# Eight-chunk Mamba and expert layer on one core: the convolution's fourth tap goes to ScalarE inside the bank, one of 13 products per chunk from GpSimd to VectorE, and two SiLU stretches become one

## The chip, the cores and the metric

One core of one Trainium2 chip. The metric is the device time of one execution in microseconds, over repeated executions. Three were taken of the kernel before: 1012.83 us in the median (1012.59 to 1013.26).

## What is computed

The input `x` has 4096 tokens of 256 numbers, in fp32 throughout. The reference is a layer norm, a Mamba block with its own RMS norm and two residual sums, then a layer norm and a mixture of eight expert networks, each for its own 512 tokens:

```python
xs, res = jnp.split(_rmsnorm(x, rms_w) @ W_in, 2, axis=-1)      # 512 channels each
xs = silu(conv_1d_depthwise(xs, conv_w, taps=4, causal) + conv_b)
dt, Bm, Cm = jnp.split(xs @ W_x, [512, 528], axis=-1)           # 16 states
dt = softplus(dt @ W_dt)
h = exp(A * dt) * h + dt * Bm * xs      # per token, 512 channels x 16 states
y = sum_n(h * Cm) * silu(res)
x = x + residual + y @ W_out
x = x + (silu(n @ w1[e]) * (n @ w3[e])) @ w2[e]                 # n = layernorm(x), e = token // 512
```

## The kernel before

**Chunks and tiles.** The tokens are cut into E = 8 chunks of TC = 512. One iteration `i` scans chunk `i`, and beside it runs the "front" of chunk `i+1` (input projection, convolution, B and C, dt) and the "back" of chunk `i-1` (gating, output projection, expert network). The scan of a chunk is Q = 32 tiles `q` of NG = 2 rows each. A row is 128 channels by 512 tokens for one state: ScalarE writes exp(A dt) to one of two PSUM banks `ebank` (line 806), VectorE runs the recurrence over it (line 664), in place in one of RING = 4 slots of `ring`, which held B times u (u = dt times xs). GpSimd multiplies the result by C (`hc`, line 513), and TensorE transposes and sums that into `ybank` (line 1133). The product B times u of a tile is made by GpSimd (line 499) for the 13 tiles in `POOL_BU` (line 34) three tiles ahead, and by VectorE (line 649) for the rest, just before the tile's scan. GpSimd reads u from SBUF, VectorE from the PSUM bank `ubank`, which ScalarE copies (line 820).

**The order of work.** Each engine executes its own list in order. The function `run` (line 306) goes over the iterations and their 32 tiles; after each tile's own work (`group`) it issues the jobs that the engine's table names for that tile. The tables are `table0` for iteration 0 and `table` for the later ones. TensorE takes its jobs from PLAN, FIRST and LAST (lines 112 to 145), and its `group` handles the tile LAG = 3 before. A job that waits holds up everything behind it on its engine, the exponentials of ScalarE and the transposes of TensorE among them.

**Banks.** Four PSUM banks `gbank` serve all other products. A loop at line 166 gives every job of the plan the bank whose last use is estimated to end first (the last number of an entry). `wait_free` waits until the job before in that bank was read, `wait_full` until the product is there.

**The convolution.** For each of the four groups `d` of 128 channels, TensorE projects into a bank ("IN"), ScalarE copies that to `xpre` (`before_conv`, line 842, two groups at tile 1 and two at tile 2), TensorE multiplies three shifted views of `xpre` by diagonal matrices into another bank ("CV", `convolve`, line 1225), and VectorE adds the fourth tap and writes `xs` (`convolved`, line 632, tiles 3, 4, 6, 6; tiles 15 to 18 in iteration 0). At tile 8 ScalarE loads the SiLU table, turns the four `xs` into SiLU in place and loads the exponential's table again (`silus`, line 871).

**Other jobs that are named below.** ScalarE: `residual` at tile 6 (line 928, four activations into the banks of "M"), `y_read` (line 894), `softplus` (line 905), `gate_silus` at tile 20 (line 1003). VectorE: `hidden(f)` at tiles 20 to 23 (line 749), which reads the bank "UP" f, `dt_of` (line 622), `gated` (line 671), `m_stats` (line 694), `x_stats` (line 616). GpSimd: `u_of` (line 481). TensorE: "DT" d (`dt_in`), "UP" f (`expand`), "DOWN" (`contract`, `contract_on`). The SiLU of the gate input `sres` (`res_silu`, line 867) runs in `gate_silus` from iteration 1 on. Those of chunks 0 and 1 run in iteration 0: that of chunk 0 in `silus_first` at tile 19, that of chunk 1 in `silus_res` at tile 24 with two table loads of its own.

## Time and profile before

| | |
|---|---|
| median of 3 executions | 1012.83 us |
| the profiled execution | 1013.09 us, of it a span of 1011.3 us in the profile |
| TensorE matmul / weight load busy | 91% / 59% |
| VectorE busy | 91% |
| ScalarE busy | 69% |
| GpSimd busy | 90% |
| mean granted TensorE clock | 0.973 of full speed |
| chain that ended last, by engine | VectorE 35%, issue 18%, TensorE 11%, GpSimd 10%, ScalarE 9% |

The three busy engines each stand near 90% over the whole span, which holds a start of about 42 us and an end of about 45 us in which only some of them have work. "Idle before" in a row is the time for which the engine did nothing before the group, and what ended it. "L664" is line 664 of the kernel.

### The profile page before, as it was taken

What the parts mean: (1) busy time and instruction counts of PE and PEld (TensorE: products, weight loads), DVE (VectorE), ACT (ScalarE), POOL (GpSimd) and SP (SyncE); (2) the same over time, 40 slices, a digit from 0 to 9 for tenths busy, and PEclk for the clock granted to TensorE, in tenths of its full rate; (3) what the DMA queues carried; (4) which work ended last, traced back from release to release, by engine and by line L of the source; (5) the groups of instructions that cost most, each with busy time, mean ns of one, the idle gap of its engine ahead of it and who ended that gap; (6) DMA issues with size and microseconds to landing.
All of it is one profiled execution on the core that took longest, in us unless ns stands there. A gap on an engine that the chain in (4) does not pass through costs nothing.

```text
span 1011.3 us, 13001 instructions
## 1 busy us (share of the span) xinstructions
PE 924.9 (91%) x4160; PEld 591.8 (59%) x4160; DVE 923.8 (91%) x1003; ACT 697.0 (69%) x1188; POOL 909.1 (90%) x499
## 2 busy tenths in 40 slices
PE   6888978999999999999999999999999997669978
PEld 4445545655756556655756557655656655555745
DVE  5789889999999999999999999999999999899941
ACT  4556777778758877778758867687758876567610
POOL 1499899999999999999999999999999999999910
PEclk9999998999999999999999999999999999779989
DMA  5590135010841039010851039110750028100200
GB/s 170 198 348 21 42 131 246 1 65 3 329 172 43 24 129 372 2 66 0 312 190 42 25 112 343 47 65 1 288 214 25 21 99 320 42 21 1 87 22 21
DMA packets 42852, 117.86 MB, mean 117 GB/s; under 512 B 8608, under 2 KB 27040, under 8 KB 32672
## 3 DMA queue, kind: packets, MB, share of 16 engines
q1 hardware_dynamic: 40928, 116.99, 30.9%
q8 instruction: 33, 0.54, 0.2%
q10 hardware_dynamic: 1856, 0.04, 0.1%
q14 instruction: 35, 0.29, 0.1%
HBM read 110.21 MB, written 6.82 MB: 116 GB/s over the span
## 4 chain that ended last, share of the span: by engine, by line
DVE 35%; issue 18%; PE 11%; POOL 10%; ACT 9%; DVEq 0%; POOLq 0%; ACTq 0%
DVE ring L664 24%; DVE ring L649 8%; POOL hc L513 7%; PE gbank L1070 4%; PE gbank L1084 3%; POOL ring L499 3%; ACT ebank L806 2%; PE ybank L1133 2%; ACT hb L1008 1%; DVE dt_ L629 1%; ACT L1011 1%; ACT L1004 1%; PE gbank L1194 1%; DVE hb L753 1%; DVE sres L676 1%
## 5 line engine op out<-in xcount | busy, mean ns | idle before, releaser
L664 DVE TENSOR_TENSOR_SCAN ring<-ebank,state,ring 128x512 f32<-128x512 f32 x512 | 623.5, 1267 | 28.0 <-ACT ebank L806 19.7
L513 POOL TENSOR_TENSOR hc<-ring,c_all 128x1024 f32<-128x1024 f32 x255 | 599.0, 2368 | 22.6 <-DMA c_all<-bc_kept 11.0
L806 ACT ACTIVATE ebank<-dt_,a_neg 128x512 f32<-128x512 f32 x512 | 349.6, 689 | 218.5 <-DVE ring L664 216.7
L1133 PEld LDWEIGHTS ybank<-ident,hc 128*128 128x128 f32 x2048 | 236.8, 143 | 105.2 <-issue 62.8
L1133 PE MATMUL ybank<-ident,hc 128*128 128x128 f32 x2048 | 262.0, 277 | 24.7 <-POOL hc L513 12.4
L499 POOL TENSOR_TENSOR ring<-b_all,u 128x1024 f32<-128x1024 f32 x103 | 243.9, 2368 | 2.3 <-ACT state L810 2.3
L649 DVE TENSOR_TENSOR ring<-b_all,ubank 128x1024 f32<-128x1024 f32 x151 | 180.5, 1195 | 1.7 <-ACT ubank L820 1.7
L1070 PE MATMUL gbank<-xT,w 128*128 128x512 f32 x320 | 150.7, 605 | 12.3 <-DVE hb L753 11.4
L1070 PE MATMUL gbank<-xT,w_a 128*128 128x512 f32 x256 | 118.5, 601 | 6.2 <-DVE dt_ L629 4.0
L1070 PE MATMUL gbank<-xs,w_a 128*128 128x512 f32 x224 | 101.0, 595 | 0.0
L1070 PEld LDWEIGHTS gbank<-xT,w 128*128 128x128 f32 x320 | 57.1, 193 | 64.5 <-issue 51.5
L1084 PE MATMUL gbank<-w2s,hb 128*128 128x256 f32 x336 | 84.4, 394 | 2.5 <-DVE hb L753 2.5
L1070 PEld LDWEIGHTS gbank<-xT,w_a 128*128 128x128 f32 x256 | 46.6, 192 | 52.3 <-issue 43.6
L1070 PE MATMUL gbank<-xpre,cdiag 128*128 128x512 f32 x168 | 76.0, 595 | 0.7 <-ACT xpre L825 0.7
L1084 PEld LDWEIGHTS gbank<-w2s,hb 128*128 128x128 f32 x336 | 60.5, 193 | 18.2 <-issue 11.9
L1070 PEld LDWEIGHTS gbank<-xs,w_a 128*128 128x128 f32 x224 | 41.0, 190 | 46.0 <-issue 46.0
L1084 PE MATMUL gbank<-wout,sres 128*128 128x256 f32 x224 | 52.9, 391 | 11.3 <-ACT gbank L937 11.3
L1084 PEld LDWEIGHTS gbank<-wout,sres 128*128 128x128 f32 x224 | 42.7, 196 | 18.4 <-issue 12.8
L1070 PEld LDWEIGHTS gbank<-xpre,cdiag 128*128 128x128 f32 x168 | 30.1, 189 | 32.0 <-issue 32.0
L486 POOL TENSOR_TENSOR u<-dt_,xs 128x512 f32<-128x512 f32 x31 | 39.6, 1279 | 0.9 <-DVE dt_ L629 0.9
L1070 PE MATMUL gbank<-xs,wbc 128*32 128x512 f32 x64 | 29.0, 595 | 0.0
L1078 PE MATMUL gbank<-ident,xin 128*128 128x128 f32 x120 | 18.6, 297 | 9.2 <-ACT xin L833 8.0
(135 smaller groups left out, 752.1 us busy)
## 6 DMA issues: line engine op xcount, KB each, us to landing
b_all<-bc_kept SPq DMA_DIRECT2D x32, 1024.0 KB, 7.2
c_all<-bc_kept SPq DMA_DIRECT2D x32, 1024.0 KB, 8.3
w<-in_L_ffn_w_dram SPq DMA_DIRECT2D x16, 640.0 KB, 4.9
w_a<-wc_kept SPq DMA_DIRECT2D x7, 1024.0 KB, 4.8
w_a<-win_kept SPq DMA_DIRECT2D x6, 1024.0 KB, 8.9
w2s<-in_L_ffn_w_dram SPq DMA_DIRECT2D x8, 640.0 KB, 4.5
xin<-in_L_attn_x_dram SPq DMA_DIRECT2D x9, 512.0 KB, 3.5
x<-in_L_attn_x_dram SPq DMA_DIRECT2D x7, 512.0 KB, 7.2
```

The costliest lines, as they stand in the source:

```text
L486: u_ok.by(e.tensor_tensor(u[:, d, :], dt_[:, d, :], xs[:, d, :], ALU.mult))
L499: bup_ok.by(e.tensor_tensor(ring[:, q % RING, :, :], b_all[:, n:n + NG, :], u[:, d, :].unsqueeze(1).broadcast_to([P, NG, TC]), ALU.mult))
L513: ch_ok.by(e.tensor_tensor(hc[:, q % HC, :, :], ring[:, q % RING, :, :], c_all[:, n:n + NG, :], ALU.mult))
L629: read_out(e.scalar_tensor_tensor(dt_[:, d, :], bank[:, :], 0.0, xpre[:, d, HALO:HALO + TC], ALU.max, ALU.add), i, "DT", d)
L649: bud_ok.by(e.tensor_tensor(ring[:, q % RING, :, :], b_all[:, n:n + NG, :], ubank[:, :].unsqueeze(1).broadcast_to([P, NG, TC]), ALU.mult))
L664: h_ok.by(e.tensor_tensor_scan(row, ebank[j % 2][:, :], row, initial=state[:, q, n:n + 1], op0=ALU.mult, op1=ALU.add))
L676: read_out(e.tensor_tensor(mine, bank[:, :], mine, ALU.mult), i, "YT", d)
L806: e_ok.by(e.activation(ebank[j % 2][:, :], dt_[:, d, :], ACT.Exp, scale=a_neg[:, d, k:k + 1]))
L1070: last = e.matmul(out_ap, a, b, start=(n == 0), stop=(n == len(terms) - 1))
L1078: return e.matmul(bank[:, cols(b)], src, ident[:, :], is_transpose=True, start=(b == 0), stop=(b == NT - 1), skip_group_check=True)
L1084: last = e.matmul(out_ap, a, b, start=False, stop=(n == len(terms) - 1), skip_group_check=True)
L1133: last = e.matmul(ybank[:, cols(b)], hc[:, q % HC, n, cols(b)], ident[:, :], is_transpose=True, start=(k == 0 and n == 0 and b == 0), stop ...
```

## The change

`convolved` moves from VectorE to ScalarE. `before_conv` now also scales the bank in place by the fourth tap after copying it, TensorE adds the other three products on top in the same bank (so "CV" no longer takes a bank of its own, and the plan's "CV" entries only say when it is read), and ScalarE copies the sum to `xs`. Tile 7 leaves `POOL_BU`. In iteration 0 `silus_res` is gone; its SiLU runs in `silus` of iteration 1. The plan and the tables are written anew around that. The core of the diff:

```diff
-    POOL_BU = (1, 4, 6, 7, 10, 12, 15, 18, 19, 22, 25, 26, 29)
+    POOL_BU = (1, 4, 6, 10, 12, 15, 18, 19, 22, 25, 26, 29)
...
         PLAN = [
-            (0, "front", "IN", 0, 1.4), (0, "front", "IN", 1, 2.2), (0, "front", "IN", 2, 2.4), (1, "front", "IN", 3, 0.5),
-            (2, "front", "CV", 0, 2.7), (3, "front", "CV", 1, 5.2), (4, "back", "YT", 3, 5.4), (4, "front", "CV", 2, 8.2),
+            (0, "front", "IN", 0, 2.4), (0, "front", "IN", 1, 0.5), (1, "front", "IN", 2, 1.4), (2, "front", "IN", 3, 2.2),
+            (2, "front", "CV", 0, 2.7), (3, "front", "CV", 1, 5.2), (4, "back", "YT", 3, 5.4), (4, "front", "CV", 2, 9.2),
...
-            (18, "back", "TAIL", 0, 23.5), (18, "scan", "YT", 1, 21.5), (18, "back", "UP", 0, 21.3), (20, "back", "UP", 1, 22.2),
-            (21, "back", "UP", 2, 22.4), (22, "back", "UP", 3, 22.7), (23, "front", "DT", 1, 25.3), (24, "back", "UP", 4, 23.4),
+            (18, "back", "TAIL", 0, 23.5), (18, "scan", "YT", 1, 21.5), (18, "back", "UP", 0, 21.3), (19, "back", "UP", 1, 22.2),
+            (21, "back", "UP", 2, 22.4), (22, "front", "DT", 1, 25.3), (23, "back", "UP", 3, 22.7), (24, "back", "UP", 4, 23.4),
...
         for i in range(-1, E + 1):
+            added = {k: until for _, _, name, k, until in plan(i) if name == "CV"}
...
+                if name == "CV":
+                    continue
...
+                    if name == "IN" and i >= 0:
+                        made[b] += 1
+                        PLACE[of, "CV", k] = b, made[b]
+                        out_at[b] = i * Q + added[k]
...
-            table = [(2, "scan", u_of(ND - 1)), (8, "back", back), (16, "handed", hand_on), (16, "front", u_of(0)),
-                     (20, "next", front), (29, "front", u_of(1)), (31, "front", u_of(2))]
-            table0 = [(5, "late", u_of(1)), (6, "late", u_of(2)), (10, "late", u_of(3)), (22, "handed", hand_on),
-                      (23, "next", front), (26, "front", u_of(0)), (27, "front", u_of(1)), (31, "front", u_of(2))]
+            table = [(0, "scan", u_of(ND - 1)), (8, "back", back), (16, "front", u_of(0)), (19, "handed", hand_on),
+                     (20, "next", front), (27, "front", u_of(1)), (31, "front", u_of(2))]
+            table0 = [(5, "late", u_of(1)), (6, "late", u_of(2)), (10, "late", u_of(3)), (23, "handed", hand_on),
+                      (25, "next", front), (26, "front", u_of(0)), (29, "front", u_of(1)), (31, "front", u_of(2))]
...
-            def convolved(d):
-                def job(c, i):
-
-                    u_ok.wait(e, c - 1, d + 1)
-                    bank = wait_full(e, i, "CV", d)
-                    read_out(e.scalar_tensor_tensor(xs[:, d, :], xpre[:, d, HALO:HALO + TC], cw[:, d, HALO:TAPS], bank[:, :], ALU.mult, ALU.add),
-                             i, "CV", d)
-                return job
...
-            table = [(3, "front", convolved(0)), (4, "back", gated(ND - 1)), (4, "front", convolved(1)),
-                     (6, "front", convolved(2)), (6, "front", convolved(3)), (8, "back", m_stats), (14, "scan", gated(0)),
-                     (17, "front", dt_of(0)), (20, "next", x_stats), (20, "scan", gated(1)), (20, "back", hidden(0)),
-                     (20, "back", hidden(1)), (20, "back", hidden_tail), (21, "back", hidden(2)), (22, "back", hidden(3)),
-                     (23, "back", hidden(4)), (24, "front", dt_of(1)), (27, "front", dt_of(2)), (28, "ahead y", gated(2)),
+            table = [(4, "back", gated(ND - 1)), (8, "back", m_stats), (15, "scan", gated(0)), (17, "front", dt_of(0)),
+                     (20, "next", x_stats), (20, "scan", gated(1)), (20, "back", hidden(0)), (20, "back", hidden_tail),
+                     (20, "back", hidden(1)), (21, "back", hidden(2)), (23, "back", hidden(3)), (23, "back", hidden(4)),
+                     (24, "front", dt_of(1)), (27, "ahead y", gated(2)), (27, "front", dt_of(2)), (30, "scan y", gated(2)),
...
             table0 = [(0, "late", fed), (2, "late", dt_of(1)), (7, "late", dt_of(2)), (9, "late", dt_of(3)),
-                      (15, "front", convolved(0)), (16, "front", convolved(1)), (17, "front", convolved(2)),
-                      (18, "front", convolved(3)), (19, "next", x_stats), (19, "scan", gated(0)), (22, "scan", gated(1)),
+                      (19, "scan", gated(0)), (20, "next", x_stats), (23, "scan", gated(1)), (28, "front", dt_of(0)),
...
-                        move("IN", d, i, xpre[:, d, HALO:HALO + TC])
+                        bank = wait_full(e, i, "IN", d)
+                        e.activation(xpre[:, d, HALO:HALO + TC], bank[:, :], ACT.Copy)
+                        read_out(e.activation(bank[:, :], bank[:, :], ACT.Copy, scale=cw[:, d, HALO:TAPS]), i, "IN", d)
+                return job
+
+            def convolved(d):
+                def job(c, i):
+                    u_ok.wait(e, c - 1, d + 1)
+                    move("CV", d, i, xs[:, d, :])
                 return job
...
                 xs_silus(c, i)
-                e.preload_act_table_set(LOG_EXP)
-
-            def silus_res(c, i):
-                e.preload_act_table(ACT.Silu)
-                res_silu(c, i)
+                if i == 1:
+                    res_silu(c - 1, i - 1)
                 e.preload_act_table_set(LOG_EXP)
...
-            table = [(1, "front", before_conv(0, 1)), (2, "front", before_conv(2, 3)), (3, "back", y_read(ND - 1)),
-                     (6, "back", residual), (8, "front", silus), (9, "back", m_copy), (10, "scan", y_read(0)),
+            table = [(1, "front", before_conv(0, 1)), (2, "front", before_conv(2, 3)), (3, "front", convolved(0)),
+                     (3, "back", y_read(ND - 1)), (4, "front", convolved(1)), (6, "front", convolved(2)), (6, "back", residual),
+                     (7, "front", convolved(3)), (8, "front", silus), (9, "back", m_copy), (10, "scan", y_read(0)),
...
-            table += [(24, "back", down_on(0)), (26, "back", down_on(1)), (28, "back", down_out(0)), (30, "ahead", residual),
+            table += [(24, "back", down_on(0)), (25, "back", down_on(1)), (30, "back", down_out(0)), (30, "ahead", residual),
...
-                      (19, "front", res(0, 1)), (19, "scan", y_read(1)), (20, "front", res(2, 3)), (22, "front", bc_read),
-                      (24, "front", softplus(0)), (24, "front", silus_res), (26, "front", softplus(1)), (26, "scan", y_read(2)),
+                      (19, "front", silus_first), (19, "scan", y_read(1)), (20, "front", res(0, 1)), (21, "front", res(2, 3)),
+                      (22, "front", bc_read), (25, "front", softplus(0)), (26, "front", softplus(1)), (27, "scan", y_read(2)),
...
-                    bank = wait_free(e, i, "CV", d)
-                    filled(product(bank[:, :], [(cdiag[:, d, k, :], xpre[:, d, k:k + TC]) for k in range(TAPS - 1)]), i, "CV", d)
+                    bank = gbank[PLACE[i, "CV", d][0]]
+                    filled(add_on(bank[:, :], [(cdiag[:, d, k, :], xpre[:, d, k:k + TC]) for k in range(TAPS - 1)]), i, "CV", d)
...
-            table += [(26, "back", contract_on(0)), (29, "back", contract_on(1))]
+            table += [(27, "back", contract_on(0)), (28, "back", contract_on(1))]
```

With these entries the loop that gives out banks puts "DT" 2 of a later iteration in the bank that "UP" 3 leaves, as before.

## Rows read from the trace of the kernel before

**Rows 1.** Busy time in stretches; columns: stretch, length, PE, PEld, DVE, ACT, POOL, clock.

```profile
347.60:462.00 114.40, 111.65 (x511) 70.79 (x510) 112.47 (x120) 87.06 (x149) 113.75 (x61) 1.00 0.33 126
...
577.10:692.20 115.10, 112.11 (x503) 70.67 (x501) 112.24 (x120) 86.49 (x149) 113.51 (x62) 0.99 0.34 125
```

**Rows 2.** Groups by line: busy us, mean ns of one, idle before them.

```profile
L664 DVE TENSOR_TENSOR_SCAN ring<-ebank,state,ring 128x512 f32<-128x512 f32 x512 | 623.5, 1267 | 28.0 <-ACT ebank L806 19.7 <-POOL ring L499 4.9
L513 POOL TENSOR_TENSOR hc<-ring,c_all 128x1024 f32<-128x1024 f32 x255 | 599.0, 2368 | 22.6 <-DMA c_all<-bc_kept 11.0 <-DVE ring L664 9.4 <-PE ybank L1133 2.1
...
L499 POOL TENSOR_TENSOR ring<-b_all,u 128x1024 f32<-128x1024 f32 x103 | 243.9, 2368 | 2.3 <-ACT state L810 2.3
...
L649 DVE TENSOR_TENSOR ring<-b_all,ubank 128x1024 f32<-128x1024 f32 x151 | 180.5, 1195 | 1.7 <-ACT ubank L820 1.7
...
L637 DVE SCALAR_TENSOR_TENSOR xs<-xpre,cw,gbank 128x512 f32<-128x512 f32 x28 | 20.0, 732 | 0.0
...
L1024 ACT ACTIVATE xs<-gbank,cw 128x512 f32<-128x512 f32 x4 | 2.7, 687 | 2.8 <-PE gbank L1070 2.8
```

**Rows 3.** Waits from 347.6 to 462 us: who waited for whom, us, times, longest.

```profile
ACT ebank L806 <- DVE ring L664: 24.7, 38, 2.9
...
DVE ring L664 <- ACT ebank L806: 1.2, 2, 0.7
...
DVE ring L664 <- POOL ring L499: 0.3, 1, 0.3
```

**Rows 4.** VectorE's timeline, a later iteration: start, us, what, idle before.

```profile
366.33 0.68 DVE L753 TENSOR_TENSOR hb<-hb,gbank 128x512 f32<-128x512 f32 x1
...
394.02 4.79 DVE L664 TENSOR_TENSOR_SCAN ring<-ebank,state,ring 128x512 f32<-128x512 f32 x4
...
416.04 1.38 DVE L637 SCALAR_TENSOR_TENSOR xs<-xpre,cw,gbank 128x512 f32<-128x512 f32 x2
417.34 2.45 DVE L664 TENSOR_TENSOR_SCAN ring<-ebank,state,ring 128x512 f32<-128x512 f32 x2
```

**Rows 5.** ScalarE's timeline beside them.

```profile
395.39 0.69 ACT L806 ACTIVATE ebank<-dt_,a_neg 128x512 f32<-128x512 f32 x1 [2.14 <-DVE ring L664]
...
397.13 1.06 ACT L825 ACTIVATE xpre<-gbank 128x512 f32<-128x512 f32 x2
398.08 1.46 ACT L806 ACTIVATE ebank<-dt_,a_neg 128x512 f32<-128x512 f32 x2
...
414.54 2.03 ACT L937 ACTIVATE gbank<-x,kept 128x256 f32<-128x256 f32 x4
416.50 1.28 ACT L806 ACTIVATE ebank<-dt_,a_neg 128x512 f32<-128x512 f32 x2
```

**Rows 6.** TensorE's timeline beside them.

```profile
353.83 1.98 PE L1070 MATMUL gbank<-xT,w 128*128 128x512 f32 x4 [1.75 <-DVE hb L753]
...
365.14 3.60 PE L1070 MATMUL gbank<-xs,w_a 128*128 128x512 f32 x8
...
392.32 5.32 PE L1070 MATMUL gbank<-xT,w_a 128*128 128x512 f32 x12
397.47 1.04 PE L1133 MATMUL ybank<-ident,hc 128*128 128x128 f32 x8
```

**Rows 7.** Iteration 0: VectorE's timeline.

```profile
69.69 1.22 DVE L649 TENSOR_TENSOR ring<-b_all,ubank 128x1024 f32<-128x1024 f32 x1 [1.70 <-ACT ubank L820]
...
139.66 4.81 DVE L664 TENSOR_TENSOR_SCAN ring<-ebank,state,ring 128x512 f32<-128x512 f32 x4 [4.39 <-ACT ebank L806]
```

**Rows 8.** Iteration 0: GpSimd's timeline, the first piece after a wait.

```profile
125.32 4.71 POOL L513 TENSOR_TENSOR hc<-ring,c_all 128x1024 f32<-128x1024 f32 x2 [0.66 <-DVE ring L664]
```

**Rows 9.** Iteration 0: ScalarE's timeline, the SiLU that moves.

```profile
135.65 1.91 ACT L869 ACTIVATE sres<-sres 128x2048 f32<-128x2048 f32 x1
```

**Rows 10.** TensorE's timeline where the iteration of 115.1 us begins.

```profile
582.90 3.38 PE L1070 MATMUL gbank<-xT,w 128*128 128x512 f32 x4 [2.10 <-DVE hb L753]
```

**Rows 11.** Waits from 806 to 965 us (iteration 7).

```profile
DVE ring L664 <- POOL ring L499: 2.4, 2, 1.6
```

More of the change, by code:

```diff
@@ new lines, in _ @@
+            table0 = [(0, "late", fed), (2, "late", dt_of(1)), (7, "late", dt_of(2)), (9, "late", dt_of(3)),
+                      (19, "scan", gated(0)), (20, "next", x_stats), (23, "scan", gated(1)), (28, "front", dt_of(0)),
+                      (28, "front", dt_of(1)), (29, "front", dt_of(2)), (30, "scan", gated(2)), (30, "front", dt_of(ND - 1))]
+            last = [(2, "back", last_c), (3, "back", gated_last), (3, "back", add_rows("M", 0, x1a_ok)),
+                    (4, "back", add_rows("M", 1, x1a_ok)), (4, "back", x1_stats), (4, "back", normal_last),
+                    (5, "back", turned_last), (5, "back", hidden_last), (12, "back", add_last)]
```

36 lines of the change are left out of this document (16 added, 20 removed), and 6 rows, old and new, of the table FIRST.

## The prediction

> **What bounds the kernel now.** I read the span in stretches first. In a later iteration GpSimd is busy for 113.75 us of 114.40, VectorE for 112.47 and TensorE for 111.65, ScalarE for 87.06 [rows 1]. So three engines are full and one has room. The waits of that iteration say how much slack is left: VectorE waits for ScalarE's exponentials for 1.2 us in two places (0.7 and 0.5, behind the two SiLU stretches) and for a product of GpSimd for 0.3 [rows 3]; GpSimd waits for nothing. VectorE and GpSimd bound an iteration together, so relief of one alone is worth nothing. The change relieves both, and pays with ScalarE.
>
> ScalarE's room is not free time. It has two banks for its exponentials, so each has a moment at which it must begin. In the timelines, a scan starts at 394.02 and the exponential two rows on starts 1.37 us later, at 395.39 [rows 4, 5]; a scan starts 0.84 us after its exponential (416.50 to 417.34) [rows 4, 5]. Scans follow each other at 1.18 us (4.79 for four, less 0.1 overlap) [rows 4]. Two scans give 2.37 us; 1.37 + 0.84 of them are taken. A job between two pairs of exponentials is free only up to about 0.75 us, plus whatever else VectorE does between those scans.
>
> **Prices.** Rows overlap by about 0.1 us at their ends, so steps are shorter than durations.
> - VectorE's fourth tap: two in 1.30 us (416.04 to 417.34), 0.65 each [rows 4]; its group has 28 at 732 ns [rows 2].
> - A product of B and u: 2368 ns on GpSimd, 1195 ns on VectorE [rows 2]; steps of 2.32 and 1.23, since the scan behind it waits for its end.
> - ScalarE's plain copy: two in 0.95 us (397.13 to 398.08), 0.48 each [rows 5]. Its copy with a per-channel scale, from a bank to SBUF, took 687 ns [rows 2]; the exponential, which has such a scale and writes to a bank, 0.69 [rows 5]. The in-place scaling of a bank isn't in the trace. It lies between 0.48 (plain copy) and 0.69 (no overlap); I take 0.60, by the scaled rows less the overlap.
>
> The rows show no difference between a bank and SBUF as the destination. The Trainium skill (ScalarE: Activation LUTs, "Step-by-step: what each stage is for") holds that ScalarE writes faster to PSUM than to SBUF; by that the 28 scalings would come nearer to 0.48, and the stalls below would shrink by about 0.2 us per iteration.
>
> **An iteration from 1 to 6, by load.** VectorE loses 4 × 0.65 = 2.6 us, gains 1.23, and saves 0.1 where `gated(0)` now stands behind a product: −1.47. GpSimd loses 2.32. ScalarE gains 4 × (0.60 + 0.48) = 4.3 us, which its 27 us of idle time could hold [rows 1]. TensorE issues the same matmuls; that three of them add to a filled bank I cost at nothing, bounded by 0 and 0.1 us. SP's transfers wait for the same events; the one behind the last "DOWN" comes one tile earlier.
>
> **The same iteration, by order.** Let 0 be the first scan of tile 0 (394.02).
> - TensorE first. VectorE read "UP" 4 at 366.33 [rows 4]. `hidden(3)` now stands just ahead of it and nothing of it is left at tile 22, so `hidden(3)` begins near 365.9 and ends near 366.5. "DT" 2 needs its bank; it began at 365.14 before [rows 6] and so begins 1.4 us later. From there to the projection at 392.32 TensorE showed no pause [rows 6], so "IN" 0 begins at 393.7, that is −0.3.
> - With 0.43 us per matmul of 512 columns (12 in 5.15) and 0.87 for a tile's eight transposes [rows 6]: "IN" 1 is full at 3.2, "IN" 2 at 5.7, "IN" 3 (behind one more tile than before) at 8.4, "CV" 0 at 11.0, "CV" 1 at 14.4.
> - ScalarE, tile 1: exponentials until 3.1, then two pairs of copy and scale, 2.16 us, until 5.3. The next exponential should begin by 5.1: **stall 0.14**.
> - Tile 2: the second pair waits for "IN" 3 and ends at 9.5 instead of 8.8. Tile 3's scans could begin at 9.7, and begin at 10.3: **stall 0.64**.
> - Tile 3: `convolved(0)` waits for "CV" 0 until 11.0, then `y_read`: 12.0, 0.1 late: **stall 0.08**.
> - Tile 6: `convolved(2)` (0.48) stands ahead of `residual` (1.96, 414.54 to 416.50 [rows 5]), where VectorE has 1.23 us of cover instead of the 1.30 of two taps: **stall 0.55**.
> - Tile 7: `convolved(3)` and the copy of `ubank` fit below the product of tile 8.
>
> New stalls 1.41 against −1.47, and the 0.3 us of waiting for GpSimd goes, as GpSimd has 2.3 us less to do: −0.3 per iteration, six times **−1.9 us**. Late next is ScalarE, held by TensorE.
>
> **Iteration 0.** GpSimd reaches `u_of(1)` one product (2.3 us) earlier, so VectorE's 1.70 us at 69.69 goes [rows 7]. VectorE's 4.39 us at 139.66 are `silus_res`: a SiLU of 1.91 us [rows 9] between two table loads. It goes too [rows 7]. But from 125.32 on GpSimd has work without a long pause until the iteration's end [rows 8], so that what VectorE gains at 139.66 shows only as far as the ring lets it lead. Of 1.70 + 4.39 = 6.1 us at least the first part comes out, since it lies before GpSimd's full stretch, and at most the whole. I take the middle, **−4.0**, bounds −1.7 and −6.1.
>
> **Iteration 1** gets that SiLU into the stretch at tile 8, which VectorE waits out already: **+1.8**, or nothing if VectorE arrives late.
>
> **Iteration 7** has no front. VectorE waits for GpSimd for 2.4 us, 1.6 of it for the product of tile 7 [rows 11]. VectorE makes that itself in 1.23, and the other 0.8 goes: about −1.1. A pause for TensorE's output projection takes 0.2 back: **−0.9**. LAST keeps each engine's order: 0.
>
> Sum: −4.0 + 1.8 − 1.9 − 0.9 = −5.0. From the profiled execution's 1013.09 us: 1008.1. That one stands 0.26 above the median of 1012.83, so **1007.8**; its own range is 1005 to 1010.5 (the scaling's bounds are ±1.2, iteration 0 ±2.2).
>
> **Rivals** (0.2%, 2 us, is about what a measurement of this kernel can tell from no change).
> - TensorE on time (0.20): it makes up the 1.4 us before tile 0. Then "IN" 3 and "CV" 0 are full when wanted and only 0.14 + 0.57 remain: −1.0 per iteration, **1003.6**. For it: "IN" 3 would come 0.7 us before it is wanted. Against: no pause in [rows 6].
> - GpSimd's pace (0.05): if ScalarE's stalls fall where VectorE would wait anyway, each iteration gains the full 2.3 us, **about 996**. Against it, VectorE is full too [rows 1].
> - Slower, by TensorE's clock (0.15). Every iteration TensorE waits for `hidden(0)`: 1.75 us at 353.83, and the four matmuls behind took 1.98 [rows 6]. Once it waited 2.10 us and they took 3.38 [rows 10], a granted clock of 1.2 in place of 2.4 GHz, and that iteration took 115.1 us instead of 114.4 [rows 1]. The change puts a second wait (1.4 us, "DT" 2) behind the first. If the clock falls in each of six iterations, the 0.7 us come back, and some 1.0 more, as ScalarE now waits for "IN" 3 in order: +1.4 each, 8.3 − 3.1 = 5.2: **1018**. It decides from 0.5 us per iteration.
> - Nothing (0.15): the stalls eat the gain of every iteration, and what iteration 0 saves comes back with iteration 1's SiLU: **1011 to 1013**. Part of the change would still do what it says.
> - The forecast has 0.45.
>
> The Trainium skill (TensorE: Matmul & The Clock Gate, "What's actually happening") says that the array runs at half rate by default and only activity releases it. The trace agrees: [rows 10] is the slow stretch behind a wait. [...]
>
> The range 1003.0 to 1013.0 takes in the forecast, TensorE on time and nothing, and leaves out 0.2. Faster 0.70 (forecast, the two faster rivals), same 0.15, slower 0.15.
>
> **What would show it.** No row of a scalar-tensor product into `xs` on VectorE; 28 scalings in a bank near 0.69 us; 95 products on GpSimd, 159 on VectorE. VectorE's waits for `ebank` in an iteration rise from 1.2 to about 2.6 us, with new ones near tiles 3 and 7; ScalarE's copies to `xpre` wait for TensorE; GpSimd waits for VectorE by some 2 us. A period near 114.1. The forecast is wrong if the period falls to 113.4 (TensorE on time), or rises with a clock below 1.00 in each iteration.

## The result, and the profile after it

The changed kernel took 1025.79 us (median of 4 runs, 1022.86 to 1026.95) against 1013.05 us for the kernel before beside it, a recorded ratio of 1.0103 with a 95% interval of [1.0081, 1.0126]: **slower by 1%**, where 1007.8 us and faster had been forecast. (The quotient of the two medians, of four runs each, is 1.0126, at the upper end of that interval; all ratios below are the recorded ones.) The profiled execution took 1022.86 us with a span of 1021.1, so it is 9.8 us longer in span than the profiled one before (1011.3).

In the comparisons below the kernel before took anything from 1012.5 to 1018.3 us, most of it probably in the first chunk (last section), so kernels are compared by ratio within one batch, and by the period of the later iterations.

The page of the changed kernel, busy time and the chain that ended last (by engine, by line):

```profile
PE 926.7 (91%) x4160; PEld 591.3 (58%) x4160; DVE 918.0 (90%) x983; ACT 721.3 (71%) x1242; POOL 890.5 (87%) x491
...
PE 58%; issue 11%; ACT 10%; DVE 10%; POOL 9%; DMA 0%; DVEq 0%; POOLq 0%; ACTq 0%
PE gbank L1072 23%; PE gbank L1086 17%; PE ybank L1135 13%; DVE ring L662 6%; POOL hc L520 5%; POOL ring L506 3%; ACT ebank L801 2%; DVE ring L647 2%; PE gbank L1080 2%; ACT hb L1008 2%; DVE hb L751 1%; ACT L1011 1%; ACT L1004 1%; ACT yt L902 1%; PE gbank L1196 1%
```

The chain now runs through TensorE for 58% of the span; through VectorE for only 10%. L1072 are the projections, L1086 the accumulating products (the convolution, the output projection and the down projection), L1135 the sums of the 16 states into y.

The changed kernel's groups by line. The scalings in a bank are there (28, 666 ns), GpSimd has 95 products and VectorE 159, and no row of VectorE writes `xs` from a bank, as the change says:

```profile
L506 POOL TENSOR_TENSOR ring<-b_all,u 128x1024 f32<-128x1024 f32 x95 | 225.1, 2369 | 0.8 <-ACT state L805 0.8
L647 DVE TENSOR_TENSOR ring<-b_all,ubank 128x1024 f32<-128x1024 f32 x159 | 190.1, 1196 | 0.0
...
L844 ACT ACTIVATE gbank<-gbank,cw 128x512 f32<-128x512 f32 x28 | 18.7, 666 | 0.0
```

**Where the 9.8 us are.** ScalarE loads its SiLU table at L1004 at tile 20 of every iteration from 1 to 7; the distance from one load to the next is the period. Starts in us, from the timelines:

```
before  233.31 347.59 462.04 576.67 692.25 806.53 920.44  end 1011.3
after   230.21 346.59 462.98 579.36 695.75 812.13 929.10  end 1021.1
```

Up to the first load the changed kernel is 3.1 us ahead. In the next five intervals it loses 8.7 us (581.92 against 573.22), in the sixth, which holds most of iteration 7, 3.1 us (116.97 against 113.91), and behind the last load 1.1. Sum: −3.1 + 8.7 + 3.1 + 1.1 = 9.8.

A later iteration of the changed kernel in one stretch, which answers to [rows 1] (stretch, length, busy time of PE, PEld, DVE, ACT, POOL, clock, DMA share, GB/s):

```profile
346.60:463.00 116.40, 111.50 (x509) 70.53 (x508) 111.62 (x117) 90.90 (x158) 111.52 (x61) 1.00 0.33 124
```

VectorE is busy 0.85 us less than in [rows 1], GpSimd 2.23 us less, TensorE the same, at a clock of 1.00; the iteration is 2 us longer. Relief of two engines came, and none of it shows. The waits of that iteration say who is held, beside [rows 3]:

```profile
ACT ebank L801 <- DVE ring L662: 16.5, 30, 1.4
...
DVE ring L662 <- ACT ebank L801: 3.3, 6, 0.8
POOL hc L520 <- PE ybank L1135: 3.3, 1, 3.3
...
PE gbank L1072 <- DVE hb L751: 3.0, 2, 1.6
ACT xs L820 <- PE gbank L1086: 2.5, 2, 2.3
...
PE ybank L1135 <- ACT yt L902: 1.9, 2, 1.2
```

GpSimd and ScalarE wait for TensorE, VectorE waits for ScalarE, and TensorE waits in four places. These are its four waits in its timeline (start, length, what, idle before), beside [rows 6]:

```profile
352.82 1.98 PE L1072 MATMUL gbank<-xT,w 128*128 128x512 f32 x4 [1.59 <-DVE hb L751]
...
365.68 3.67 PE L1072 MATMUL gbank<-xs,w_a 128*128 128x512 f32 x8 [1.39 <-DVE hb L751]
...
378.20 1.09 PE L1135 MATMUL ybank<-ident,hc 128*128 128x128 f32 x8 [0.69 <-ACT yt L902]
...
402.24 2.74 PE L1086 MATMUL gbank<-xpre,cdiag 128*128 128x512 f32 x6
406.22 1.10 PE L1135 MATMUL ybank<-ident,hc 128*128 128x128 f32 x8 [1.24 <-ACT yt L902]
```

1.59 + 1.39 + 0.69 + 1.24 = 4.91 us, and 111.50 + 4.91 = 116.41: these four are all of its idle time. That sum alone proves nothing, since the busy and the idle time of any engine add up to the period. What tells who holds the iteration is the chain of work followed back through it (start, length, what):

```profile
365.68 3.67 PE gbank L1072 x8
...
377.55 0.61 ACT yt L902
...
378.20 1.09 PE ybank L1135 x8
...
405.57 0.60 ACT yt L902
...
406.22 1.10 PE ybank L1135 x8
...
456.81 0.89 PE ybank L1135 x8
```

From 365.7 to 457.7 us it doesn't leave TensorE but for the two copies of y that TensorE itself waits for; the 19 us before that are ScalarE's SiLU and the scans behind it. In the kernel before, the same stretch of the chain never touches TensorE: it runs over the SiLU and VectorE up to 406 us and over GpSimd from 407.5 on. So **TensorE bounds the changed iteration, through the order of its own queue**. The waits are:

- 1.59 us for `hidden(0)`, which the kernel before has too (1.75, [rows 6]).
- 1.39 us: "DT" 2 needs the bank that `hidden(3)` reads, and `hidden(3)` now stands at tile 23.
- 0.69 us: y of tile 24 needs `ybank`, which `y_read(2)` empties. `contract_on(0)`, which stood in front of it at tile 26, is now at tile 27.
- 1.24 us: y of a new chunk needs `ybank`, which `y_read(3)` empties, and on ScalarE that now stands behind `convolved(0)`, which waits for TensorE.

The kernel before had one more wait, which the rows ahead don't show and which is gone from the changed kernel:

```profile
415.72 3.69 PE L1084 MATMUL gbank<-wout,sres 128*128 128x256 f32 x16 [1.00 <-ACT gbank L937]
```

There TensorE came too early for `residual` at tile 6: 111.65 + 1.75 + 1.00 = 114.40. The iteration grew by the new waits, 1.39 + 0.69 + 1.24 = 3.32 us, less the 1.00 at the residual, less 0.16 at `hidden(0)` and 0.15 of busy time: 2.0 us.

ScalarE's timeline at the last of them (beside [rows 5]):

```profile
397.05 0.58 ACT L843 ACTIVATE xpre<-gbank 128x512 f32<-128x512 f32 x1
397.52 0.65 ACT L844 ACTIVATE gbank<-gbank,cw 128x512 f32<-128x512 f32 x1
398.10 0.60 ACT L843 ACTIVATE xpre<-gbank 128x512 f32<-128x512 f32 x1
...
405.08 0.60 ACT L820 ACTIVATE xs<-gbank 128x512 f32<-128x512 f32 x1 [0.21 <-PE gbank L1086]
405.57 0.59 ACT L902 ACTIVATE yt<-ybank 128x512 f32<-128x512 f32 x1
...
409.99 0.60 ACT L820 ACTIVATE xs<-gbank 128x512 f32<-128x512 f32 x1 [2.28 <-PE gbank L1086]
```

The copy to `xs` at 405.08 waits until TensorE has filled the bank; `yt` follows at 405.57, and TensorE, idle, goes on at 406.22. TensorE waits for ScalarE, which has just waited for TensorE. The first three rows also give the price of a scaling: 397.52 to 398.10, 0.58 us.

### The profile page after: what moved, and what is told of

Same layout as the page of the kernel before. It is cut to its first block, busy times and chain, and to the rows that moved or that the text cites. A ratio compares the mean times of both kernels' runs of the same rounds, so it can differ in the third digit from the quotient of the medians.

```text
span 1021.1 us, 13000 instructions
## 1 busy us (share of the span) xinstructions
PE 926.7 (91%) x4160; PEld 591.3 (58%) x4160; DVE 918.0 (90%) x983; ACT 721.3 (71%) x1242; POOL 890.5 (87%) x491
## 4 chain that ended last, share of the span: by engine, by line
PE 58%; issue 11%; ACT 10%; DVE 10%; POOL 9%; DMA 0%; DVEq 0%; POOLq 0%; ACTq 0%
PE gbank L1072 23%; PE gbank L1086 17%; PE ybank L1135 13%; DVE ring L662 6%; POOL hc L520 5%; POOL ring L506 3%; ACT ebank L801 2%; DVE ring L647 2%; PE gbank L1080 2%; ACT hb L1008 2%; DVE hb L751 1%; ACT L1011 1%; ACT L1004 1%; ACT yt L902 1%; PE gbank L1196 1%
## 5 line engine op out<-in xcount | busy, mean ns | idle before, releaser
L520 POOL TENSOR_TENSOR hc<-ring,c_all 128x1024 f32<-128x1024 f32 x255 | 598.8, 2369 | 50.7 <-PE ybank L1135 23.2
L801 ACT ACTIVATE ebank<-dt_,a_neg 128x512 f32<-128x512 f32 x512 | 345.9, 689 | 170.7 <-DVE ring L662 169.0
L1135 PEld LDWEIGHTS ybank<-ident,hc 128*128 128x128 f32 x2048 | 236.4, 143 | 114.0 <-issue 66.8
L1135 PE MATMUL ybank<-ident,hc 128*128 128x128 f32 x2048 | 262.2, 278 | 31.3 <-ACT yt L902 19.3
L506 POOL TENSOR_TENSOR ring<-b_all,u 128x1024 f32<-128x1024 f32 x95 | 225.1, 2369 | 0.8 <-ACT state L805 0.8
L647 DVE TENSOR_TENSOR ring<-b_all,ubank 128x1024 f32<-128x1024 f32 x159 | 190.1, 1196 | 0.0
L1072 PE MATMUL gbank<-xT,w 128*128 128x512 f32 x320 | 149.5, 601 | 11.2 <-DVE hb L751 10.3
L1072 PE MATMUL gbank<-xT,w_a 128*128 128x512 f32 x256 | 119.6, 602 | 5.5 <-DVE dt_ L636 3.9
L1072 PE MATMUL gbank<-xs,w_a 128*128 128x512 f32 x224 | 101.7, 598 | 8.3 <-DVE hb L751 8.3
L1072 PEld LDWEIGHTS gbank<-xT,w 128*128 128x128 f32 x320 | 56.8, 192 | 63.1 <-issue 51.2
L1086 PE MATMUL gbank<-w2s,hb 128*128 128x256 f32 x336 | 84.3, 393 | 2.6 <-DVE hb L751 2.6
L1086 PE MATMUL gbank<-xpre,cdiag 128*128 128x512 f32 x168 | 75.7, 592 | 0.0
L1072 PEld LDWEIGHTS gbank<-xT,w_a 128*128 128x128 f32 x256 | 46.2, 192 | 47.9 <-issue 40.7
L1072 PEld LDWEIGHTS gbank<-xs,w_a 128*128 128x128 f32 x224 | 40.4, 190 | 56.6 <-issue 56.6
L1086 PEld LDWEIGHTS gbank<-w2s,hb 128*128 128x128 f32 x336 | 60.0, 192 | 18.7 <-issue 12.7
L1086 PE MATMUL gbank<-wout,sres 128*128 128x256 f32 x224 | 53.8, 396 | 5.3 <-ACT gbank L937 5.3
L1086 PEld LDWEIGHTS gbank<-wout,sres 128*128 128x128 f32 x224 | 43.6, 200 | 11.6 <-issue 5.7
L1086 PEld LDWEIGHTS gbank<-xpre,cdiag 128*128 128x128 f32 x168 | 30.6, 190 | 33.1 <-issue 33.1
L1072 PE MATMUL gbank<-xs,wbc 128*32 128x512 f32 x64 | 29.0, 595 | 0.0
L820 ACT ACTIVATE xs<-gbank 128x512 f32<-128x512 f32 x28 | 16.6, 591 | 15.1 <-PE gbank L1086 15.0
```

The source lines that it names most:

```text
L506: bup_ok.by(e.tensor_tensor(ring[:, q % RING, :, :], b_all[:, n:n + NG, :], u[:, d, :].unsqueeze(1).broadcast_to([P, NG, TC]), ALU.mult))
L520: ch_ok.by(e.tensor_tensor(hc[:, q % HC, :, :], ring[:, q % RING, :, :], c_all[:, n:n + NG, :], ALU.mult))
L647: bud_ok.by(e.tensor_tensor(ring[:, q % RING, :, :], b_all[:, n:n + NG, :], ubank[:, :].unsqueeze(1).broadcast_to([P, NG, TC]), ALU.mult))
L801: e_ok.by(e.activation(ebank[j % 2][:, :], dt_[:, d, :], ACT.Exp, scale=a_neg[:, d, k:k + 1]))
L820: ins = e.activation(dst, bank[:, :], ACT.Copy)
L1072: last = e.matmul(out_ap, a, b, start=(n == 0), stop=(n == len(terms) - 1))
```

## The experiments

The theory tested: the new waits in TensorE's queue are the whole loss. The rivals: ScalarE is overloaded; VectorE or GpSimd still bounds; the product of tile 7 is on the wrong engine; the first chunk's SiLU matters. "Waits" below are TensorE's in one later iteration; "period" is the distance of the loads at tile 20.

| kernel | ratio to before [95%] | waits of TensorE, us | period, us | chain in it: TensorE, VectorE, GpSimd |
|---|---|---|---|---|
| before | 1 | 1.75 + 1.00 = 2.75 | 114.3 to 115.6 | 0%, 31%, 29% |
| changed | 1.0103 [1.0081, 1.0126] | 1.59 + 1.39 + 0.69 + 1.24 = 4.91 | 116.39 | 77%, 6%, 0% |
| 1: `y_read(3)` first | 1.0056 [1.0035, 1.0077] | 1.59 + 1.38 + 0.69 + 0.46 = 4.12 | 115.60 | 76%, 6%, 0% |
| 2: `hidden(3)` back | 1.0021 [1.0003, 1.004] | 1.59 + 0.89 + 1.23 = 3.71 | 114.96 | 68%, 14%, 0% |
| 3: both | 0.9974 [0.9953, 0.9995] | 1.59 + 0.89 + 0.46 = 2.94 | 114.18 | 66%, 14%, 0% |
| 5: 3 and `contract_on` back | 0.9942 [0.9921, 0.9963] | 1.59 + 0.87 = 2.46 | 113.73 | 45%, 26%, 0% |
| 6: 5 and `convolved(2)` later | 0.9944 [0.9921, 0.9966] | 1.59 + 0.87 = 2.46 | 113.73 | 45%, 26%, 0% |
| 7: only tile 7 moved | 1.0077 [1.0054, 1.01] | 2.09 + 0.99 + 0.57 = 3.65 | 115.4 or 116.7 | 0%, 60%, 0% |
| 8: only the convolution | 1.0012 [0.9996, 1.0029] | 1.92 + 0.72 = 2.64 | 115.35, once 114.43 | 33%, 30%, 8% |
| 9: 5 with tile 7 on GpSimd | 1.0002 [0.9979, 1.0024] | 1.95 + 0.87 = 2.82 | 114.1 to 114.8 | 31%, 7%, 41% |

The waits and the chain are those of iteration 2 in each profiled execution (in the kernel before, the one of 114.4 us). In 2, 5 and 6 the first of the five periods is 1.0 to 1.5 us longer than the one given, with slow rows behind `hidden(0)` (last section).

The times that were expected of 1 to 3 go by 1013 us for the kernel before, which took 1016.8 us in their batch, so they are read as gains on the changed kernel: about 7, 5 to 8, and 13 to 16 us. The ratios give some 4.8, 8.3 and 13.1 us. The first gained less than expected (its wait shrank and didn't go), the second just over its range, the third came out at its lower end; "no change", the rival's, is out for all three.

The period less the waits is 111.48, 111.48, 111.25, 111.24 and 111.27 us in the changed kernel and in 1, 2, 3 and 5. That is TensorE's busy time. It would be so whoever bounded the kernel; what counts is that a wait taken out didn't come back in full elsewhere in TensorE's queue, and that the period fell with it.

**1, the last `y_read` ahead of `convolved(0)`** (on the changed kernel):

```diff
-(3, "front", convolved(0)),
-(3, "back", y_read(ND - 1)), (4, "front", convolved(1)),
+(3, "back", y_read(ND - 1)),
+(3, "front", convolved(0)), (4, "front", convolved(1)),
```

> The changed kernel, but ScalarE's y_read(3) stands ahead of convolved(0) at tile 3. Theory (TensorE's waits in order): the copy to xs waits for CV 0 and holds y_read(3), for which TensorE then waits 1.24 us; that goes in six iterations, so about 7 us less than the changed kernel, near 1018 us. Rival (ScalarE has too much to do): the same two jobs in another order, no change, near 1025 us.

Measured: 1021.16 us, ratio 1.0056. The wait of 1.24 us became 0.46 and the period fell by the same 0.79 us. Swapping two instructions of ScalarE, with its load unchanged, is worth 4.7 thousandths.

**2, `hidden(3)` and its bank a tile earlier** (on the changed kernel):

```diff
-(22, "front", "DT", 1, 25.3), (23, "back", "UP", 3, 22.7)
+(22, "back", "UP", 3, 22.7), (23, "front", "DT", 1, 25.3)
...
-(23, "back", hidden(3)), (23, "back", hidden(4))
+(22, "back", hidden(3)), (23, "back", hidden(4))
```

> The changed kernel with UP 3 and hidden(3) back at tile 22 and DT 1 at 23. Theory: TensorE's wait of 1.39 us for hidden(3) goes in each of six iterations, 5 to 8 us less than the changed kernel, 1018 to 1020 us. Rival (ScalarE has too much to do): its jobs are the same, no change, near 1025 us.

Measured: 1017.64 us, ratio 1.0021. The wait of 1.39 us is gone, 0.20 of it came back at the next one (0.69 to 0.89), and the period fell by 1.43, 1.20 by the waits and 0.23 by TensorE's busy time.

**3, both edits together.**

> Both edits. Theory: both waits go, 13 to 16 us less than the changed kernel, 1009 to 1012 us, unless VectorE becomes the bound before that. Rival (ScalarE): near 1025 us.

Measured: 1014.17 us, ratio 0.9974. The two gains add: 0.79 + 1.43 = 2.22, and the period fell by 2.21. In one queue two waits add up; ScalarE's overload, the rival, is out, since ScalarE does the same work in the changed kernel and in all three of these.

**4, the kernel before with the SiLU of the first chunk moved to iteration 1.**

```diff
                 xs_silus(c, i)
+                if i == 1:
+                    res_silu(c - 1, i - 1)
                 e.preload_act_table_set(LOG_EXP)
...
- (24, "front", silus_res),
```

> The kernel before, with only the SiLU of chunk 1 moved from its own stretch in iteration 0 into the stretch at tile 8 of iteration 1. Theory of the prediction: 2.3 to 4.4 us less in iteration 0, 1.8 more in iteration 1, so 1010.5 to 1012.5 us. Rival (GpSimd holds iteration 0's end, so nothing comes out there): 1013 to 1014.6 us.

Measured: 1016.76 us, ratio 1.0003 [0.9983, 1.0023]. Alone it changes nothing that can be measured, and the trace shows why: with the SiLU gone from iteration 0, ScalarE waits there for TensorE's sum of y instead, and VectorE still stands 3.86 us (it was 4.39, [rows 7]).

```profile
147.72 0.60 ACT L899 ACTIVATE yt<-ybank 128x512 f32<-128x512 f32 x1 [3.37 <-PE ybank L1130]
149.00 2.46 DVE L664 TENSOR_TENSOR_SCAN ring<-ebank,state,ring 128x512 f32<-128x512 f32 x2 [3.86 <-ACT ebank L806]
```

**5, `contract_on` back as well** (on 3):

```diff
-table += [(27, "back", contract_on(0)), (28, "back", contract_on(1))]
+table += [(26, "back", contract_on(0)), (29, "back", contract_on(1))]
```

> Edit: the third experiment's kernel (last y_read ahead of convolved(0), UP 3 a tile earlier and DT 1 a tile later) plus contract_on(0) back at tile 26 and contract_on(1) at 29. Theory (TensorE's waits in its order are the cost): in the third experiment TensorE still waits 0.89 us for yt of y_read(2), because contract_on(0) no longer stands in front of that product. With it back the wait falls to 0.3 us or less, 0.6 us per iteration times six, so 3 to 4 us off the third experiment: ratio to before 0.9935 to 0.997. Rival (VectorE and GpSimd are the bound again after the third experiment, so TensorE's wait is covered): ratio 0.9965 to 0.9985, as the third experiment, the TensorE wait merely moving elsewhere.

Measured: 1010.45 us, ratio 0.9942. The wait for `yt` at tile 24 is gone, 0.41 of its 0.89 us came back at the next `yt` (0.46 to 0.87), and the period fell by 0.45 to 113.73. The intervals of 3 and 5 overlap; it is the traces that tell them apart, by the period and by the stretch behind the last load, which is 2.0 us shorter (90.7 us against 92.7). The same iteration in a stretch, and TensorE's only two waits in it:

```profile
347.90:461.60 113.70, 111.22 (x509) 70.69 (x508) 111.18 (x117) 91.10 (x158) 111.55 (x61) 1.00 0.33 126
```

```profile
354.15 1.98 PE L1072 MATMUL gbank<-xT,w 128*128 128x512 f32 x4 [1.59 <-DVE hb L751]
...
404.89 1.09 PE L1135 MATMUL ybank<-ident,hc 128*128 128x128 f32 x8 [0.87 <-ACT yt L902]
```

TensorE no longer holds the whole iteration. The chain leaves ScalarE's SiLU at 356 us, runs over VectorE's scans to 396.8, crosses ScalarE at tiles 1 to 3 and only from 404.9 to 456.4 us is on TensorE. With every part of the change in it, this kernel is faster than both.

**6, `convolved(2)` behind the residual** (on 5):

```diff
-(6, "front", convolved(2)), (6, "back", residual), (7, "front", convolved(3))
+(6, "back", residual), (7, "front", convolved(2)), (7, "front", convolved(3))
```

> Edit: the fifth experiment's kernel plus convolved(2) at tile 7, behind the residual instead of ahead of it at tile 6. The prediction priced that place at 0.55 us of VectorE per iteration, and the trace of the changed kernel shows 0.56. Theory A (VectorE is again a bound once TensorE's waits are gone): up to 0.5 us per iteration, 3 us off the fifth experiment, ratio 0.991 to 0.995. Theory B (TensorE is the bound at 111.5 us of work per iteration plus its waits): nothing, ratio as the fifth experiment within 0.001, though the row with the 0.56 us stall on VectorE is gone.

Measured: 1010.16 us, ratio 0.9944, as 5. The stall on VectorE (0.55 us in 5, 0.56 in the changed kernel) is gone from the trace and the period stays at 113.73. So a stall that the prediction had priced to 0.01 us is worth nothing here: at 416.97 us of run 5 it lies where the chain is on TensorE. It doesn't show that VectorE has room everywhere, since up to 396.8 us the chain is on VectorE.

**7, tile 7's product taken from GpSimd, and nothing else** (on the kernel before):

```diff
-POOL_BU = (1, 4, 6, 7, 10, 12, 15, 18, 19, 22, 25, 26, 29)
+POOL_BU = (1, 4, 6, 10, 12, 15, 18, 19, 22, 25, 26, 29)
```

> Edit: the kernel before with tile 7 taken out of POOL_BU, nothing else: GpSimd has 2.32 us less per iteration, VectorE 1.23 us more. If VectorE and GpSimd bound an iteration together (the prediction's reading), VectorE's 1.23 us lengthens it by 0.6 to 1.2 us: ratio 1.003 to 1.008. If TensorE's order alone set the period of before, the ratio is 1.000 within 0.002.

Measured: 1023.71 us, ratio 1.0077 [1.0054, 1.01]. Two iterations in stretches (columns as above; the second is one with the clock at 0.99):

```profile
353.20:468.70 115.50, 111.83 (x511) 70.83 (x510) 113.75 (x121) 87.13 (x151) 111.74 (x61) 1.00 0.33 124
468.70:585.40 116.70, 113.14 (x510) 71.59 (x509) 113.86 (x121) 86.94 (x150) 111.72 (x61) 0.99 0.34 123
```

Here VectorE bounds: busy 113.75 of 115.50, 1.28 more than in [rows 1], and the iteration is longer by 1.1. The chain of the first of the two goes over VectorE for 60% and over GpSimd and TensorE for nothing. In the kernel before VectorE had no room for 1.23 us, as the prediction read.

**8, the new convolution alone** (on the kernel before: scaling in the bank, three taps added on top, ScalarE's copy to `xs`, "IN" 2 and 3 one tile later, and the last `y_read` ahead of `convolved(0)`; GpSimd keeps 13 products):

```diff
-bank = wait_free(e, i, "CV", d)
-filled(product(bank[:, :], [(cdiag[:, d, k, :], xpre[:, d, k:k + TC]) for k in range(TAPS - 1)]), i, "CV", d)
+bank = gbank[PLACE[i, "CV", d][0]]
+filled(add_on(bank[:, :], [(cdiag[:, d, k, :], xpre[:, d, k:k + TC]) for k in range(TAPS - 1)]), i, "CV", d)
...
-move("IN", d, i, xpre[:, d, HALO:HALO + TC])
+bank = wait_full(e, i, "IN", d)
+e.activation(xpre[:, d, HALO:HALO + TC], bank[:, :], ACT.Copy)
+read_out(e.activation(bank[:, :], bank[:, :], ACT.Copy, scale=cw[:, d, HALO:TAPS]), i, "IN", d)
```

> Edit: the kernel before with the in-bank scaling and ScalarE's copy into xs, TensorE adding three taps on top (IN 2 and IN 3 one tile later, the last y_read ahead of convolved(0)), with 13 products on GpSimd and the old order of hidden, contract and the SiLU. VectorE loses 2.6 us per iteration, GpSimd keeps its 113.75 us. Theory (the loop TensorE, ScalarE, TensorE through the copies costs little where the last y_read is ahead; GpSimd holds the period): ratio 0.998 to 1.001. Rival (the convolution's hand-over itself is the slow part: scaling and copies hold ScalarE, ScalarE holds the scans): ratio 1.005 or more, with VectorE waiting for ScalarE more than 2.5 us per iteration.

Measured: 1016.62 us, ratio 1.0012 [0.9996, 1.0029], just over the upper end that the theory gave and below the rival's 1.005, although VectorE waits for ScalarE's exponentials for 3.1 us in the first iteration below, over the 2.5 that the rival named: waits of that size cost little here.

```profile
347.40:462.80 115.40, 112.76 (x511) 71.61 (x509) 110.54 (x116) 90.77 (x159) 113.97 (x63) 0.99 0.34 125
578.10:692.50 114.40, 111.62 (x512) 70.84 (x510) 110.16 (x116) 91.05 (x158) 113.75 (x62) 1.00 0.34 126
```

VectorE is busy 2 us less than in [rows 1], GpSimd as before: 113.75 us in an iteration of 114.40, which leaves it 0.65, and what VectorE gained is lost. Only one of the five periods was 114.43. The other four were 115.35, with slow matmuls behind `hidden(0)` (last section), and in the stretch of 115.40 the chain goes over TensorE for 38 us from those matmuls on.

**9, tile 7 back on GpSimd** (on 5):

```diff
-POOL_BU = (1, 4, 6, 10, 12, 15, 18, 19, 22, 25, 26, 29)
+POOL_BU = (1, 4, 6, 7, 10, 12, 15, 18, 19, 22, 25, 26, 29)
```

> Edit: the fifth experiment's kernel with tile 7 back in POOL_BU (GpSimd makes 13 products an iteration, as before), everything else as there. The fifth experiment's period is 113.73 us, its GpSimd busy 111.95 and its VectorE 111.58. Theory (with the tap off VectorE, GpSimd's 113.75 us plus the waits it has anyway bound the iteration): period 114.3 or more, 0.5 to 0.9 us per iteration on six or seven, ratio to before 0.998 to 1.001, that is 3 to 6 us over the fifth experiment. Rival (TensorE's 111.6 us plus its waits of 2.5 us hold the period, GpSimd has the room): ratio as the fifth experiment, 0.993 to 0.996, and the move of tile 7 is worth nothing even then.

Measured: 1015.58 us, ratio 1.0002 [0.9979, 1.0024]; periods 114.09 to 114.84.

```profile
346.40:460.80 114.40, 111.56 (x512) 70.70 (x510) 110.13 (x116) 91.18 (x157) 113.75 (x62) 1.00 0.34 126
```

GpSimd is at its 113.75 us again, and it has the largest part of the chain, 41%. With the kernel before, runs 7, 9 and 5 make four corners (7 has the orders of the kernel before, 9 and 5 the mended ones and the moved SiLU): the product's move alone +0.8%, the convolution without the move 0.0% (run 9; run 8, with the old order elsewhere, +0.1%), both −0.6%. Neither half is worth anything without the other.

**10 and 11, the order around `hidden(0)` put back** (on 5): "UP" 1 at tile 20, and in 11 also `hidden_tail` behind `hidden(1)`.

```diff
-(19, "back", "UP", 1, 22.2),
+(20, "back", "UP", 1, 22.2),
...
-(20, "back", hidden_tail), (20, "back", hidden(1))
+(20, "back", hidden(1)), (20, "back", hidden_tail)
```

> Edit: the fifth experiment's kernel with UP 1 put back from tile 19 to tile 20, behind the wait for hidden(0). In the fifth experiment TensorE waits 1.59 us for hidden(0) in each of iterations 3 to 7 and the four matmuls behind take 1.98 (full clock). In the eighth experiment the wait was 1.90 to 2.11 us, and they took 2.4 to 3.7 in five of six. Theory (a longer wait lets the clock fall): if this edit lengthens the wait to 1.9 us or more, rows of 2.4 to 3.4 us appear behind it and each such iteration takes 0.9 to 1.3 us longer: ratio to before 0.996 to 1.000. Rival (the length of this wait has nothing to do with the clock): waits near 1.9 with rows of 1.98, or slow rows behind waits of 1.59; ratio 0.993 to 0.996.

> Edit: as the tenth, and hidden_tail behind hidden(1) again, as in the kernel before. This changes VectorE's order at tile 20 too. Theory (a longer wait lets the clock fall): the wait for hidden(0) as in the kernel before or the eighth experiment, 1.75 to 2.1 us, slow rows in one to five of six iterations, ratio to before 0.995 to 1.000. Rival (no tie between the wait and the clock): ratio 0.993 to 0.996 with rows of 1.98 behind waits of any of these lengths.

Measured: 1010.11 us, ratio 0.9942 [0.992, 0.9964], and 1008.12 us, 0.9927 [0.9899, 0.9956]. **Inconclusive on their question**: neither edit moved the wait for `hidden(0)`, which stayed at 1.57 to 1.59 us in iterations 2 to 6 with rows of 1.98 behind it, so neither could show what a longer wait does. Their periods are 113.7, as in 5, and the intervals of all three overlap.

## Why the prediction was wrong

**The step that failed** is "the same iteration, by order", where it closes: "new stalls 1.41 against −1.47". It took VectorE's account, counted from the first scan of tile 0, for the iteration's. The prediction found the 1.4 us by which "DT" 2 comes late (measured: 1.39), followed it to the next projection as "−0.3" (measured: 393.62 against a first scan at 393.93), and priced only what ScalarE and VectorE lose behind it. That the stretch from tile 20 to that first scan grows too it put at nothing: it grew from 46.43 to 47.34 us, and the rest of the iteration, for which the prediction's own terms give −0.4, by 1.0. The two other waits, 0.69 and 1.24, weren't found at all: the prediction didn't follow who is in front of `y_read(3)` on ScalarE and who waits for it, nor what `contract_on(0)` had covered at tile 26.

The rows ahead of the prediction held a warning. TensorE's one spare wait, 1.00 us for the residual, stands at tile 6 of the next chunk, and a late TensorE reaches the other engines before that, through the copies of the transposed x at the end of the iteration. The slow iteration of [rows 10] shows it. The four matmuls took 3.38 us instead of 1.98, and the chain goes on from them over TensorE to that copy:

```profile
582.90 3.38 PE gbank L1070 x4
...
620.40 0.45 PE gbank L1078 x4
620.88 0.46 ACT xT L825
```

For those 1.40 us the iteration paid 0.9 to 1.3 us (115.58 us from load to load, against 114.28 to 114.64), although 0.89 us of the wait for the residual was left. The prediction read the same iteration in stretches as 115.1 against 114.4, so as 0.7 us, and had the price too low. In run 7 matmuls that took 1.3 us longer cost 1.3 us. So a delay of TensorE at tile 20 had 0.5 us of room at most, and the new wait of 1.4 us for "DT" 2 comes a few tiles later in the same queue.

Point by point:

- **What bounds the kernel.** Right as far as it went: VectorE and GpSimd together (runs 7, 8, 9). Incomplete: the chain changes hands within an iteration, VectorE to 406 us and GpSimd behind it, and TensorE is a third, 0.5 us or less behind from tile 20 on.
- **Prices.** Right. Scaling 0.58 us by its step (0.60 taken, 0.48 to 0.69 given), copy 0.47 (397.05 to 397.52; 0.48 taken), products 2369 and 1196 ns. That a bank as destination is the faster one, which the Trainium skill (ScalarE: Activation LUTs, "Step-by-step: what each stage is for") holds, shows as 21 ns at most: 666 ns for the scaling in a bank against 687 from a bank to SBUF [rows 2].
- **ScalarE's stalls.** Nearly right, and worth nothing. VectorE waits 3.3 us for `ebank`, where about 2.6 was forecast; the stall at tile 6 is there (0.56, forecast 0.55), that of tile 3 too (0.84, forecast 0.64), and at tile 1 about 0.1 (forecast 0.14). The timetable behind them held as well, up to "CV" 0, which is full 11.1 us behind the first scan (forecast 11.0); "CV" 1 came at 16.0, 1.6 late (forecast 14.4), behind TensorE's wait of 1.24 for `y_read(3)`. Run 6 took one of these stalls out for no gain.
- **Iterations 0 and 1.** Right in sign: −3.1 us up to tile 20 of iteration 1, against −4.0 + 1.8 = −2.2. The first stall, 1.70 us at 69.69 [rows 7], is gone from the changed kernel's trace, as forecast; run 9, with tile 7 on GpSimd, shows 1.71 us there again, and its first load comes 1.7 us after that of run 11 (232.28 against 230.59 us). The second, 4.39 us, was read as the SiLU's. It wasn't only that: run 4 takes the SiLU away and gains nothing, as told there. The 1.8 us for iteration 1 showed as a stall of 2.26 us at 195.23. How the rest adds up is open.
- **Iterations 2 to 6.** Wrong: 8.7 us lost, about 1.6 gain forecast. This is the most of the error. (The forecast's own terms, 1.41 − 1.47 − 0.3 = −0.36, give −2.2 for six iterations, where it wrote −1.9; nothing hangs on that.)
- **Iteration 7.** Wrong: 3.1 us lost in the interval that holds it, 0.9 gain forecast. Two of TensorE's new waits fall in it, at the end of iteration 6, and the output projection (16 matmuls, L1086) ran slower than in the kernel before. TensorE's timeline in the changed kernel:

```profile
831.23 3.67 PE L1072 MATMUL gbank<-xs,w_a 128*128 128x512 f32 x8 [1.40 <-DVE hb L751]
843.75 1.09 PE L1135 MATMUL ybank<-ident,hc 128*128 128x128 f32 x8 [0.69 <-ACT yt L902]
...
880.86 6.64 PE L1086 MATMUL gbank<-wout,sres 128*128 128x256 f32 x16 [5.05 <-ACT gbank L937]
```

The same projection in the kernel before:

```profile
873.34 5.44 PE L1084 MATMUL gbank<-wout,sres 128*128 128x256 f32 x16 [5.49 <-ACT gbank L937]
```

  1.40 + 0.69 + (6.64 − 5.44) = 3.3 us, close to the 3.1. The granted clock was 0.50 and then 0.60 over the longer one, and 0.50 and then 0.92 over the shorter. No run was made for this sum, but it comes out in others too. In run 1 the projection took 5.41 us, the two waits stayed, and the sum is 2.1 of 1.9 us lost; in run 5 both waits are gone, the projection took 6.33 and twelve matmuls of L1072 took 6.32 instead of 5.32, and the sum is 1.9 of 2.0. What makes these matmuls slow in one kernel and not in the other is open.
- **Behind the last load.** 1.1 us lost, where nothing was forecast. It goes with `contract_on`: the stretch is 90.8 us in the kernel before, 92.0 to 93.0 in the four kernels that have it at tiles 27 and 28 (changed, 1, 2, 3), and 90.7 to 91.1 in the eight others.
- **The rivals.** "Slower, by TensorE's clock" named the right engine and sign (1018 us) and the wrong mechanism: the granted clock was 1.00 in the later iteration, and each group of four matmuls behind the wait for `hidden(0)` took 1.98 or 1.99 us. "GpSimd's pace" is refuted: GpSimd waits 3.3 us for TensorE. "Nothing" is refuted too, as the kernel lost 1%. "TensorE on time", 1003.6, wasn't reached by any run. With mended orders 0.9942 of 1012.83 would be 1007.0, next to the forecast's 1007.8; that is luck, since it takes three orders that the forecast didn't ask for, and its period of 113.7 is not the 114.1 of the forecast.

## What to carry to other kernels

For each engine that is nearly full, list the waits in its own queue. Busy time and waits always add up to the period, so the sum shows nothing; ask which of the waits shrinks when the engine is late, and whether the engine hands something over ahead of it. Only a delay behind the last such hand-over is free: here TensorE had a spare wait of 1.00 us, and a delay ahead of it still cost nearly its full length. A new wait is to be held against that room, not against the engine's share of busy time. Follow the chain through one iteration, and note where it changes engines: a stall that is taken out off the chain gains nothing (run 6). When work moves between engines, walk every queue that it is moved into and ask what is now behind it and which engine waits for that; a consumer placed ahead of the copy that frees its producer's bank makes a loop of two engines that wait for each other in turn. Where two engines bound together, test the halves of a change together: here the halves alone gave nothing or a loss, and both with three orders mended gave 0.6%.
